# Attention products from stacked high and low parts in one fp32r pass, all slot sums on TensorE, row counts on ScalarE

## What is computed

```python
# layer 1: agg = segment_sum(relu(h[src] @ conv_w + conv_b), dst); layer 2 needs out_deg (row counts)
w_m = (efeat @ W_msg + b_msg).reshape(E, 16, 16)
w_a = (efeat @ W_attn + b_attn).reshape(E, 16, 16)
h_src = feat[src][:, :, None]
e1, e2 = w_m * h_src, w_a * h_src
ex = exp(e2 - segment_max(e2, dst)[dst])
ft = segment_sum(e1 * ex / segment_sum(ex, dst)[dst], dst)
x = x + ft.sum(axis=1)
```

## Time and profile before

| | us |
|---|---|
| median of 3 runs (2711.42 to 2713.04) | 2711.72 |
| span of the profiled execution (no other time of it is given) | 2774.5 |
| PE, DVE, ACT busy in it | 2191.1, 2233.7, 1763.9 |
| attention loop in it, about | 1190 to 2700 |
| mean granted TensorE clock in it | 0.847 |

### The profile page before, as it was taken

The page is one execution under the profiler, slowest core; times in us unless marked ns, Lnnn a source line. Parts: engine busy times, 40 slices in busy tenths (PEclk is TensorE's granted clock), DMA queues, the critical chain, the costliest instruction groups (busy, mean ns, idle before and its releaser), DMA issues. The chain is left out here.

```text
span 2774.5 us, 36642 instructions
## 1 busy us (share of the span) xinstructions
PE 2191.1 (79%) x7895; PEld 960.2 (35%) x7896; DVE 2233.7 (81%) x3857; ACT 1763.9 (64%) x6869; POOL 1321.9 (48%) x1141
## 2 busy tenths in 40 slices
PE   1688888898699984488888888888888888888870
PEld 0344444466455532123222222222222222222220
DVE  7799999314587702399999999999999999999996
ACT  6577777013111111588888888888888888888843
POOL 5000000405550002577767777677777777777704
PEclk9899999888899996588888888888888888888885
DMA  3000000205785431012222222222222222222214
GB/s 69 6 0 0 0 0 0 93 1 177 244 259 179 139 116 23 19 52 71 71 71 71 71 71 71 70 63 71 71 71 71 71 71 71 71 71 71 66 57 123
DMA packets 109221, 205.35 MB, mean 74 GB/s; under 512 B 38652, under 2 KB 66980, under 8 KB 103406
## 3 DMA queue, kind: packets, MB, share of 16 engines
q1 hardware_dynamic: 67278, 156.49, 16.0%
q0 software_dynamic: 41888, 48.19, 8.0%
HBM read 76.22 MB, written 128.34 MB: 74 GB/s over the span
## 5 line engine op out<-in xcount | busy, mean ns | idle before, releaser
L1803 POOL DMA_INDIRECT hs<-h_table,gix x860 | 1081.6, 1258 | 434.5 <-issue 241.8
L1914 ACT ACTIVATE e<-wps,hs 128x32 f32<-128x32 f32 x5632 | 1030.6, 404 | 227.5 <-PE wps L1844 158.9
L1844 PE MATMUL wps<-w_edge,ef 18*128 18x512 f32 x1760 | 578.8, 706 | 301.1 <-ACT e L1914 162.6
L1866 PE MATMUL slot_sums<-e,ident 128*128 128x512 f32 x1392 | 757.0, 694 | 8.5 <-DVE e L2018 7.0
L1866 PEld LDWEIGHTS slot_sums<-e,ident 128*128 128x128 f32 x1392 | 294.8, 223 | 489.0 <-issue 463.7
L1844 PEld LDWEIGHTS wps<-w_edge,ef 18*128 18x128 f32 x1760 | 159.3, 200 | 678.1 <-ACT e L1914 309.8
L526 ACT CAST edges<-acc 128x400 f32 x600 | 295.0, 492 | 102.0 <-PE acc L513 75.3
L509 PE MATMUL acc<-q_hot,lo_hot 128*128 128x400 bf16 x1200 | 307.4, 338 | 53.3 <-DVE q_hot L483 51.4
L1953 DVE TENSOR_TENSOR e<-wps,hs 128x2048 f32<-128x2048 f32 x132 | 301.6, 2285 | 54.9 <-remote 23.0
L551 POOL DMA_INDIRECT got<-in_edge_rows,start x64 | 65.1, 1018 | 543.9 <-POOLq L464 417.6
L483 DVE TENSOR_SCALAR q_hot<-qcol,qT 128x400 bf16<-128x400 bf16 x1200 | 290.5, 317 | 1.0 <-PE acc L513 0.9
(11 more groups left out here) (381 smaller groups left out, 1964.0 us busy)
## 6 DMA issues: line engine op xcount, KB each, us to landing
rows_state<-states SPq DMA_DIRECT2D x43, 1280.0 KB
rows_shift<-shifts SPq DMA_DIRECT2D x44, 640.0 KB
got_order<-edges_order SPq DMA_DIRECT2D x56, 256.0 KB
ef_order<-efT SPq DMA_DIRECT2D x56, 256.0 KB
hs<-h_table,gix POOLq DMA_INDIRECT x880
ef<-ef_order SPq DMA_DIRECT2D x44, 320.0 KB
edges_order<-got POOLq DMA_DIRECT2D x32, 256.0 KB
edges_order<-msg_parts POOLq DMA_DIRECT2D x24, 256.0 KB
```

Source lines behind the costliest of these rows:

```text
L1803: nc.gpsimd.indirect_dma_start(out=hs[u][:, s, :], out_offset=None, in_=d["h_table"], in_offset=bass.IndirectOffsetOnAxis(ap=gix[u][:, s:s ...
L1844: nc.tensor.matmul(wps[:, bank, :], ef[u][k:k + KM, g * P:(g + 1) * P], w[k:k + KM, :], start=True, stop=True).then_inc(a_mult, 1)
L1866: ins = nc.tensor.matmul(sums[:, g % 2, :], ident[:, :], e[u][:, g * SLOTS + c, :], start=(c == 0), stop=(c == SLOTS - 1))
L1914: ins = nc.scalar.mul(e[u][:, s, at], wps[:, bank, at], hs[u][:, s, f:f + 1])
```

## The change

1. Edge features and weights are split into a high part (the low 12 bits of the float32 cleared) and the rest. The weights' split is made in `layer2` (two DVE instructions on 18x512, then four DMAs into `w_stack`). The features' split is made in `layer1_sum`, two DVE instructions of 128x512 a turn; `ef_order` becomes `ef_high` and `ef_low`, so that a turn stores two tables instead of one, and `ef` is loaded by four DMAs a block (68 partitions times 4 slots times 640 columns: 696 KB) where it was one (320 KB).
2. A product is one fp32r matmul over 68 stacked rows (high times high, high times low, low times high, low times low) for one slot, where it was a float32 matmul over 18 rows.
3. TensorE adds group 4 too (BYPE 5). DVE's `halve` and `quarter` go; `accumulate` 2 moves ahead of the subtracts of groups 3 to 0 and `accumulate` 3 ahead of the second multiply. In PE's order product 13 now stands before the products of slots 16 to 19, with the fifth sum before it.
4. Row counts of layer 1 move from DVE's strips (56 of L1343 and L1347) to ACT: 50 copies of 128x1568 with an accumulated sum.
5. `msg_parts` holds one half; the second is loaded in five pieces as PE frees the first half's; PE's inner loops are swapped. POOL's fetches get their own space. SP's and ACT's loops there are unrolled. Three semaphores of `prepare_pairs` last longer.

```diff
@@ layer1_sum, SP
+                def keep_split(turn):
+                    groups = slice(turn * TURN, (turn + 1) * TURN)
+                    sp.wait_ge(y_split, turn * 2 + 2)
+                    sp.dma_start(d["ef_high"][:, groups, :], high[turn % SPLITS][:, :, :]).then_inc(u_stored[turn % SPLITS], 16)
+                    sp.dma_start(d["ef_low"][:, groups, :], efT[turn % SPLITS][:, :, :]).then_inc(u_stored[turn % SPLITS], 16)
@@ layer1_sum, ACT
+                def outdegrees(f, t):
+                    half = slice(f * (COLS // PARTS), (f + 1) * (COLS // PARTS))
...
+                    nc.scalar.activation(junk[:, :], edges[:, t, half], ACT.Copy, accum_out=rowparts[:, t, f:f + 1]
+                                         ).then_inc(y_rows, 1)
@@ layer1_sum, DVE
-                        nc.vector.tensor_reduce(
-                            rowsum[:, :], edges[:, :, turn * SCOLS:(turn + 1) * SCOLS],
-                            X, ALU.add).then_inc(m_dve, 1)
-                        dve.wait_ge(m_dve, turn * 2 + 2)
-                        nc.vector.tensor_tensor(raw, raw, rowsum[:, :], ALU.add).then_inc(m_dve, 1)
+                        if r or j > 0:
+                            split(j * TURNS_IN_CHUNK + r - 1)
+                def split(turn):
+                    value, top = efT[turn % SPLITS], high[turn % SPLITS]
+                    dve.wait_ge(y_evac, turn + 1)
+                    nc.vector.tensor_scalar(top[:, :, :].bitcast(I32), value[:, :, :].bitcast(I32), -4096, None,
+                                            ALU.bitwise_and).then_inc(y_split, 1)
+                    dve.wait_ge(y_split, turn * 2 + 1)
+                    nc.vector.tensor_tensor(value[:, :, :], value[:, :, :], top[:, :, :], ALU.subtract
+                                            ).then_inc(y_split, 1)
@@ attention_edges
-    ORDER = [4, 5, 0, 1, 2, 3, 6, 7, 8, 9, 10, 11, 12, 16, 17, 18, 19, 13, 14, 15]
+    ORDER = [4, 5, 0, 1, 2, 3, 6, 7, 8, 9, 10, 11, 12, 13, 16, 17, 18, 19, 14, 15]
-    BYPE = 4
-    SUM_READ = (3, 4, 6, 7)
-    SUM_DONE = (2, 2, 3, 4)
+    BYPE = 5
+    SUM_READ = (5, 4, 6, 7, 8)
+    SUM_DONE = (2, 2, 3, 4, 5)
-                    sp.dma_start(ef[u][:, :], ef_t[:, cols(b, BG * P)]).then_inc(a_ef[u], 16)
+                    for at, half, rows in ((0, high_t, KM), (KM, high_t, KM), (2 * KM, low_t, F), (2 * KM + F, low_t, F)):
+                        sp.dma_start(ef[u][at:at + rows, :, :], half[0:rows, :, cols(b, BG * P)]).then_inc(a_ef[u], 16)
-                    g, k = s // SLOTS, s % SLOTS * KE
-                    nc.tensor.matmul(wps[:, bank, :], ef[u][k:k + KM, g * P:(g + 1) * P],
-                                     w[k:k + KM, :], start=True, stop=True).then_inc(a_mult, 1)
+                    g, c = s // SLOTS, s % SLOTS
+                    nc.tensor.matmul(wps[:, bank, :], ef[u][:, c, g * P:(g + 1) * P].bitcast(F32R),
+                                     w[:, :].bitcast(F32R), start=True, stop=True).then_inc(a_mult, 1)
@@ period
                     for_act(u, b, (7,))
+                    add(3)
                     for_dve(u, b, 1, NV + 1)
-                    add(3)
                     for_act(u, b, (12,))
+                    add(4)
+                    for_act(u, b, (13,))
                     for_dve(u, b, 2, NV + 2)
-                    for_act(u, b, (13, 14, 15))
+                    for_act(u, b, (14, 15))
@@ block_step
                     for g in range(2):
                         v.wait(up(v, u, g))
-                    shifted = up(v, u, 2)
-                    halve(w, 4).then_inc(a_halved, 1)
-                    v.wait(shifted)
+                    v.wait(up(v, u, 2))
                     shifted = up(v, u, 3)
...
                     subtract(u, 4)
                     next_block(0)
+                    accumulate(v, w, b - 1, 2)
                     for g in reversed(range(4)):
                         subtract(u, g)
-                    accumulate(v, w, b - 1, 2)
+                    accumulate(v, w, b - 1, 3)
                     next_block(1)
-                    dve.wait_ge(a_halved, b + 1)
-                    quarter(v, w, 4)
-                    accumulate(v, w, b - 1, 3)
                     accumulate(v, w, b - 1, 4)
                     dve.wait_ge(a_acc, b * BG + BG)
                     next_block(2)
```

More of the change, by code:

```diff
@@ L1201, in layer1_sum @@
         m_first = [sem(f"m_first{k}") for k in range(TILES // PIECE)]
-        m_load = sem("m_load")
+        m_second = [sem(f"m_second{k}") for k in range(TILES // PIECE)]
+        m_free = sem("m_free")
         m_store, m_sum, m_evac, m_dve, m_raw, m_sqrt = (sem("m_" + n) for n in "store sum evac dve raw sqrt".split())
         u_load = [sem("u_load0"), sem("u_load1")]
[L1205 to L1211, removed]
+        u_stored = [sem(f"u_stored{r}") for r in range(SPLITS)]
+        y_turned, y_evac, y_copied, y_masked, y_moved, y_split, y_rows = (
+            sem("u_" + n) for n in "turned evac copied masked moved split rows".split())
+        room = [lent[:, v, :, :] for v in range(fetch.ROOMS)]
         def left(g):
@@ L1279, in chunk @@
                     n, r = 0, 0
-                    for a in range(3):
-                        for k in range(TILES):
-                            at = j - f * CHUNKS
-                            if j == 0 and a == 0 and k % PIECE == 0:
-                                pe.wait_ge(m_first[k // PIECE], 16)
-                            ins = nc.tensor.matmul(acc[:, at, 0:CW], parts[:, f, k, a, :],
+                    at = j - f * CHUNKS
+                    for k in range(TILES):
+                        if at == 0 and k % PIECE == 0:
+                            pe.wait_ge((m_second if f else m_first)[k // PIECE], 16)
+                        for a in range(3):
+                            ins = nc.tensor.matmul(acc[:, at, 0:CW], parts[:, k, a, :],
                                                    edges[:, k, at * CW:(at + 1) * CW],
@@ L1288, in chunk @@
                             n += 1
+                            if j == SECOND and n % (3 * PIECE) == 0 and n < 3 * TILES:
+                                ins.then_inc(m_free, 1)
                             if n == (r + 1) * 3 * TILES // TURNS_IN_CHUNK - 4:
@@ L1488, in layer2 @@
             sem("r_" + s) for s in "sel dve sq sqd parts agg evac small h st blank".split())
+        r_w, r_split, r_stack = (sem("r_" + s) for s in "w split stack".split())
         def cw(n):
@@ L1713, in attention_edges @@
         sums = ctx.enter_context(nc.psum_tensor("slot_sums", [P, 2, 2 * CH], F32))
-        a_w, a_mult, a_read_v, a_read_s, a_sub, a_exp, a_weighed, a_sum, a_halved, a_acc, a_shift, a_last, a_step, a_go = (
-            sem("a_" + s) for s in "w mult read_v read_s sub exp weighed sum halved acc shift last step go".split())
+        a_mult, a_read_v, a_read_s, a_sub, a_exp, a_weighed, a_sum, a_acc, a_shift, a_last, a_step, a_go = (
+            sem("a_" + s) for s in "mult read_v read_s sub exp weighed sum acc shift last step go".split())
         a_marks, a_x = sem("a_marks"), sem("a_x")
@@ L2096, in block_step @@
                         gather_index(u, b + 2)
-                    weigh(v, w, b - 1)
+                    weigh(w, b - 1)
                     masks(v, u, b)
```

172 lines of the change are left out of this document (94 added, 78 removed).

## The result

| | before | after |
|---|---|---|
| median of 6 runs each (range), us | 2710.93 (2706.65 to 2713.04) | 2719.93 (2717.43 to 2720.91) |
| ratio, 95% interval | | 1.0033 (1.0023 to 1.0043) |
| profiled execution: its time, its span | no time given, 2774.5 | 2720.42, 2718.7 |

The change costs 9 us, 0.33%. Forecast was a gain of 31. The page of the kernel after, part 1, and its attention loop in the windows view (columns as in the earlier trace rows), beside the earlier trace rows: PE and DVE are both less busy, ACT is not.

A forecast was written before the change was run, and what follows sets the result against it. Attention loop bound by DVE to its last subtract, then ACT's five slots, 35.2 us a block. -36 us in 42 blocks at 34.35, +3.5 and +1 in layer 1: -31 scaled, 2681 us; range 2656 to 2735.

The forecast's parts named there:

- the block of before: Attention loop: 35.2 us a block, from DVE's last subtract through 1.1 us of exponential to five ACT slots of 15.3 us.
- The wait for PE: DVE's wait ahead of the first sum in the attention loop: from 0.96 us a block to 0.1.
- Path D: DVE's third multiply: starts T + 21.75 + 5x, closes block T + 32.5 + 5x (T: ACT's slot 15 read).
- S7's end: Attention loop: ACT has read slot 7, which product 13 waits for, at T + 21.55.
- Path A: Block closed by ACT's five slots after DVE's last subtract and the exponentials: T + 34.0.
- The first rival: Attention loop: DVE's third multiply eats the gain, Path D at 34.5 to 35.1; 0 to -25 us, chance 0.18.
- The price x: One stacked fp32r product on PE: 0.25 us at the high clock, 0.5 at the low one.
- Stacking against row tiling: DVE's products: four unstacked in row groups take 1.14 us, 0.285 each; stacking gains for these only below that.
- The slower rival: Product 13 ahead of 16 to 19 with x over 0.54: 2738 us at x = 0.65; chance 0.21.
- Other work in the loop: POOL's gathers take 31.2 us a block, 3.3 of wait remaining at 34.35; `ef` loads issued a block ahead: no cost.
- the rival of POOL or DMA: Gathers slowed 3 us or more hold block near 35; with full DMA in layer 1, 2695 to 2720; chance 0.07.
- Layer 1: Stage of sums: between -4 and +12 us, taken as +3.5; +1 at the stage's end.

The follow-up runs named there:

- fp32r_alone: Kernel after with stacked fp32r products kept but four sums on PE and both old orders: 2691.66 us, 0.9927 of before.
- order13: Kernel after with product 13 back behind those of slots 16 to 19, fifth sum and DVE's order kept: 2697.43 us, 0.9950 of before.
- sum2_first: order13 with the sum of group 2 added ahead of product 6 in PE's order: 2674.59 us, 0.9874 of before.
- high_only: fp32r_alone with high parts alone, 18 rows and one load of 180 KB a block: 2695.89 us, 0.9944 of before.
- before_again: Kernel before, unchanged, profiled a second time: 2709.49 us, 0.9997 of before; profiled span 2707.8 us.
- filler: Kernel after with two more float32 matmuls of 512 columns on PE ahead of product 13: 2730.92 us, 1.0065 of before.

## Why the prediction was wrong

- **The step that failed is the first: the block of before.** It read 35.2 us, closed by ACT's last slot, in the one trace given, and set every gain against it. In a second trace of the same kernel the block is 34.14 and DVE closes it. The forecast block, 34.35, was close to the measured 34.14 of after; the saving of 0.85 was the excess of that trace. Scaling the difference by 2.3% didn't mend this: the time too much was not spread over the kernel. Of the 66.7 us between the two traces 62.1 lie between the first gather and the end of the loop, along with the "issue" waits of L1914, 67.2 us; the earlier trace rows show one of them, 0.42, in the very block that was read.
- **The wait for PE.** It was 0.96 a block in that trace, 20.3 / 44 = 0.46 in the next. It went to nothing in after and in fp32r_alone, as said; in the latter it is the larger part of the 0.61 us by which the block shrinks.
- **Path D** was right in place and size: third multiply at T + 21.75 + 5x forecast, 24.25 at the low clock; measured 24.05. S7's end was forecast at T + 21.55 (product 13, which waits for it, starts at T + 21.51), and the block 35.0; it is 34.76. The share of such blocks was not: one in two, where one in three was taken.
- **Path A** was put at 34.0 from slots of 15.3 us. With 14.4 it closes at 32.88. So path D rules in every block of after, by 0.7 us even in the short ones of 33.6 (forecast for it at the high clock: 33.75), and the order of product 13 is worth 20.8 us. The first rival, that the third multiply eats the gain, had this mechanism; it too was priced on the wrong base (0 to -25 us; measured +3.4 in the loop).
- **The price x.** Forecast were 0.25 and 0.5, so 1.25 and 2.5 for the five products of path D. Of its 43 rows in after, 22 take 1.43 to 1.56 us and 21 take 2.50, so x was low by some 0.04 at the high clock. One product alone behind a wait takes 0.50 us at the high clock and 0.80 at the low one, so that each further one takes 0.23 and 0.425; a row directly behind a sum, 1.70, gives 0.225 in the same way. The Trainium skill's 215.7 and 426.7 ns for 512 columns (TensorE: Matmul & The Clock Gate, "Wait — 56ns, not 53.3ns?") are within 8% of that.
- **Stacking against row tiling.** fp32r_alone gains 25.4 us of loop though it gives up the four unstacked products side by side in 1.14 us. So the advice of the Trainium skill (TensorEngine Tiling (Array Packing), "When to Use Tiling") wasn't needed here; no run has the one format both ways, and fp32r in row groups wasn't tried.
- **The slower rival** needed x over 0.54, and didn't come.
- **The fifth sum**: from fp32r_alone to order13 the loop grows by 8.0 us. Its short blocks are 0.64 shorter, since DVE has less to do. In the long ones a sum comes late behind a product that waits for ACT (31.3 us of DVE's waits); that the added sums, 3.6 us of PE each, are why PE has no room there is an argument, not shown. sum2_first gives it back: 9.4 us less loop than fp32r_alone.
- **Other work in the loop**: nothing, as said (high_only). That also rules out the rival of POOL or DMA.
- **Layer 1**: forecast +3.5 and +1. By the means over the traces the sums take 242.4 against 240.4 us, and from their end to the first gather of attention it is 120.8 against 119.2: +2.0 and +1.6, near the forecast. That is luck in part: the gain, some 9 us, is over twice what the bound of -4 had it, the store's cost, some 11, is near the bound of +12, and they nearly cancel. DMA, forecast to be full in the first part, is at 0.90 there.

The account: the loop is +3.4 (products -25.4, fifth sum and DVE's order +8.0, product 13 ahead +20.8), layer 1 +3.6 by the means. The parts depend on the order in which they are taken: with float32 products the fifth sum and the new orders cost 18.6, with stacked ones 8.0 + 20.8 = 28.8, since path D then takes what the products gave. The two profiled spans, after and before_again, differ by 10.9: start +1.6, sums +4.5, to the first gather +2.8, to the first block -0.1, loop +3.4, the end -1.3. The first three and the end vary by 3 to 4 us from trace to trace, so that the 9 us of the medians can't be split more finely.

## What to carry to other kernels

When the only profile of a kernel is 2% longer than its runs, look for where the extra time sits before reading the bound from it: here 62.1 of 66.7 us sat in one stage, beside "issue" waits of one engine that the next trace didn't have, and had made that engine look like the bound. In an order written by hand, each in-order queue passes on the lateness of what it waits for: put the work that another engine needs soon ahead of the product that waits for a third, and measure the place again when the engines' loads change, since the same exchange took 17.4 us off the loop with five sums on PE (order13) and added 15.8 with four (fp32r_alone).

## What was not expected of the hardware

- One execution in which ACT took 67.2 us of "issue" between multiplies of 0.29 us, 1.11 us at a time ahead of the loop. None of the other traces of these kernels shows it.
- The granted clock in filler fell though PE had been at work until 1.30 us before the products (windows above): extra matmuls in a gap are no sure means to hold it.
- An fp32r product alone takes 0.80 us at the low clock, over 68 rows as over 18 (0.79, high_only), and 0.50 behind a wait at the high clock, again with both. Directly behind a sum at the high clock it takes 0.80 over 68 rows and 0.50 over 18. In a row of five, each further one takes 0.225 us for 512 columns, where a float32 matmul takes 0.925.
